# Moving the gelu and its closing table load behind the softmax exponential of slot 5

## The reference

```python
def attn_layer(x, Wqkv, qs, ksc, Wo):
    q, k, v = jnp.split(x @ Wqkv, 3, -1)          # 16 heads of 64
    q = l2norm(q) * qs
    k = l2norm(k) * ksc
    q = q * cos * scale + rotate_half(q) * sin * scale
    k = k * cos * inv + rotate_half(k) * sin * inv
    return local_attention(q, k, v) @ Wo          # windows of 32, softmax over 64 keys

def ffn_layer(x, g, bln, W1, b1, W2, b2):
    hg = layernorm(x, g, bln) @ W1 + b1
    a, gate = jnp.split(hg, 2, -1)                # 341 wide each
    return a * jax.nn.gelu(gate, approximate=False) @ W2 + b2

for i in range(DEPTH):                            # DEPTH = 6
    x = attn_layer(shift_tokens(x), ...) + x
    x = ffn_layer(shift_tokens(x), ...) + x
```

## Time and profile before

| | us |
|---|---|
| median of 3 runs | 4368.58 |
| lowest and highest of them | 4362.37, 4377.15 |
| the profiled execution, its own time | 4373.77 |
| span in that profile | 4372.0 |
| PE busy | 3763.1 |
| DVE busy | 2883.2 |
| ACT busy | 2553.7 |
| POOL busy | 1865.4 |

### The profile page before, as it was taken

How to read it: one execution, slowest core, us unless ns; L and a number is a source line. 1 busy time by engine, 2 the same in 40 slices (tenths; PEclk the granted TensorE clock), 3 DMA queues, 4 the chain that set the end, 5 groups by cost and what they waited for, 6 DMA issues and landing times. The chain is left out here.

```text
span 4372.0 us, 155161 instructions
## 1 busy us (share of the span) xinstructions
PE 3763.1 (86%) x66004; PEld 2803.9 (64%) x66004; DVE 2883.2 (66%) x4808; ACT 2553.7 (58%) x4737; POOL 1865.4 (43%) x1571
## 2 busy tenths in 40 slices
PE   5998699987898987899997899997898897898895
PEld 4997566665666665666665666665666665666663
DVE  3223677776677776777776677776677776677773
ACT  2121566665566665666665666665666665666664
POOL 1011354444444543454444454443454454454451
PEclk9676899999999999999998999999999999999997
DMA  0000110101101101111011110111101101111012
GB/s 27 6 9 23 51 30 26 30 26 36 48 27 30 30 25 41 40 30 31 26 31 41 40 30 25 30 30 37 44 27 29 30 25 41 40 30 30 26 30 68
DMA packets 91938, 139.69 MB, mean 32 GB/s; under 512 B 19465, under 2 KB 40608, under 8 KB 90400
## 3 DMA queue, kind: packets, MB, share of 16 engines
q1 hardware_dynamic: 84778, 129.84, 10.1%
q10 hardware_dynamic: 6518, 0.03, 0.1%
HBM read 28.32 MB, written 4.19 MB: 7 GB/s over the span
## 5 line engine op out<-in xcount | busy, mean ns | idle before, releaser
L1066 POOL TENSOR_TENSOR nat<-ra,rb 128x512 f32<-128x512 f32 x768 | 999.3, 1301 | 1351.7 <-DVE ra L1107 1169.5
L1070 POOL TENSOR_TENSOR nat<-nat,rr 128x512 f32<-128x512 f32 x768 | 814.8, 1061 | 689.8 <-ACT rr L1020 634.7
L1106 DVE TENSOR_TENSOR rb<-ps,tab 128x512 f32<-128x512 f32 x768 | 526.1, 685 | 454.0 <-ACT sq L977 446.7
L783 PE MATMUL ps<-wh,xls 128*128 128x512 f32 x1152 | 614.6, 534 | 217.0 <-PEq L126 188.5
L977 ACT ACTIVATE sq<-ps 128x512 f32<-128x512 f32 x768 | 447.4, 597 | 183.4 <-PE ps L785 145.8
L814 PE MATMUL ps<-kT,qT 64*32 64x64 f32 x24704 | 448.0, 220 | 88.9 <-issue 85.9
L1107 DVE TENSOR_TENSOR ra<-ps,tab 128x512 f32<-128x512 f32 x768 | 522.2, 680 | 0.0
L814 PEld LDWEIGHTS ps<-kT,qT 64*32 64x32 f32 x24704 | 371.2, 106 | 182.5 <-issue 166.1
L795 PE MATMUL ps<-con,nat 128*128 128x128 f32 x3080 | 432.4, 278 | 41.6 <-POOL nat L1070 31.4
L784 PE MATMUL ps<-wl,xhs 128*128 128x512 f32 x1152 | 466.7, 405 | 0.0
L785 PE MATMUL ps<-wh,xhs 128*128 128x512 f32 x1152 | 466.0, 405 | 0.0
(11 more groups left out here) (166 smaller groups left out, 6076.2 us busy)
## 6 DMA issues: line engine op xcount, KB each, us to landing
v<-v SPq DMA_DIRECT2D x192, 396.0 KB, 3.6
v<-v SPq DMA_DIRECT2D x96, 132.0 KB, 3.5
raw<-in_L_ffn_Wqkv SPq DMA_DIRECT2D x7, 1536.0 KB, 6.5
v<-v SPq DMA_DIRECT2D x96, 66.0 KB, 3.2
tab<-in_rotary SPq DMA_DIRECT2D x6, 512.0 KB, 3.3
raw<-in_L_ffn_Wo SPq DMA_DIRECT2D x6, 512.0 KB
xnat<-in_L_attn_hidden_states SPq DMA_DIRECT2D x8, 256.0 KB, 3.7
sT<-so SPq DMA_DIRECT2D x8, 256.0 KB, 2.0
```

The source lines that it names most:

```text
L783: nc.tensor.matmul(dst, al, bh, start=True, stop=False)
L1066: nc.gpsimd.tensor_tensor(nat[:, k, :], ra[:, k, :], rb[:, k, :], ALU.add).then_inc(cur["add"], 1)
L1070: nc.gpsimd.tensor_tensor(nk, nk, rr[:, k, :].unsqueeze(2).broadcast_to([P, 8, DH]), ALU.mult).then_inc(cur["qkn"], 1)
L1106: nc.vector.tensor_tensor(heads8(rb[:, k, :]), heads8(ps[:, bank, :])[:, :, ::-1, :], sin, ALU.mult)
```

## The change

In ScalarE's program, the gelu of slot 5, with the wait for `gx` ahead of it and the table load behind it, moves from in front of the norm's logarithm to behind the softmax exponential of the same slot. Nothing else changes: the same instructions with the same operands.

```diff
@@ -1008,10 +1008,6 @@
-                if i == 5:
-                    act.wait_ge(cur["gx"], NJ)
-                    nc.scalar.activation(gx[:], gx[:], ACT.Gelu).then_inc(cur["gl"], 1)
-                    nc.scalar.preload_act_table_set(LN_EXP)
                 if full:
                     act.wait_ge(cur["g"], i + 1)
                     nc.scalar.activation(nrm[:], nrm[:], ACT.Ln, scale=RN * RN).then_inc(cur["ln"], 1)
@@ -1029,6 +1025,10 @@
                 if live(i, 2):
                     act.wait_ge(cur["sub"], i + 1)
                     nc.scalar.activation(pr[:, i % 2, :], pr[:, i % 2, :], ACT.Exp).then_inc(cur["exp"], 1)
+                if i == 5:
+                    act.wait_ge(cur["gx"], NJ)
+                    nc.scalar.activation(gx[:], gx[:], ACT.Gelu).then_inc(cur["gl"], 1)
+                    nc.scalar.preload_act_table_set(LN_EXP)
```

## The result

Timed side by side, the changed kernel takes 4467.8 us (median of 4 runs, 4464.5 to 4471.9), the one before 4372.9 us (4362.4 to 4377.2). The ratio is 1.0221, with a 95% interval from 1.0199 to 1.0244. Timed once more, later, it was 1.0232 (1.0215 to 1.0249). The kernel is slower by about 95 us, where +82 was forecast. The kernel before stands 4.3 us higher in this timing than the 4368.6 us that the forecast starts from, so the difference is the thing to compare, not the time.

What follows compares the result with a forecast made beforehand. A ring through ScalarE, DVE and PE was taken to bound the kernel, so delays of slot 6's squares count in full: 37.5 + 33 + 11 = +82 us on 4368.6 gives 4451 us, range 4405 to 4500.

Steps and rivals of the forecast that it cites:

- three signs: Wrong if slot 6's squares wait for PE, their delay misses the round distance, or granted clock falls in most rounds.
- What bounds the kernel: Slots 5 and 6: no single engine but a ring; a delay of slot 6's squares meets no slack beyond some tenths.
- the ring: Squares on ScalarE, rotary and sums on DVE, turned output, v and next projections on PE, squares again.
- What the change removes: Slot 5: norms 2.0 us sooner, exponential at 3.39 us instead of 4.92, PE's 1.53 us wait nearly gone; off the ring.
- What it adds, the queue: ScalarE: exponential 0.66, block 4.09, `v` and `pt` 0.94, 5.69 us in sum; slot 6's squares at 9.08, delayed 1.38 us.
- What it adds, the second chain: Gelu, DVE's gated product, PE's projection of q: would allow slot 6's squares at 8.5 us, not setting the end.
- Two kinds of rounds: 28 short rounds (early subtraction) cost 37.5 us; 20 with PE stalled in slot 5's scores cost 33 and 11 us.
- The clock rival: PE's clock falls in its new idle time: 0.81 us in each of 48 rounds, +39 us, 4490; 15 in 100.
- Part given back: PE's stalls without shown cause shrink when PE comes later, giving 4422 or 4433 us; 17 in 100.
- Faster: Squares not waiting for ScalarE, PE keeps its saved wait: 61 us less, 4308; block from 2.71 down; 5 in 100.
- no change: The delay vanishes at each round's end, where engines wait on each other across the loop's jump; 4 in 100.
- The table load: Each load costs only what the block's 4.09 us shows; by the skill's 2.66 us per switch, another 131 us.

Runs made afterwards that it cites:

- up_sooner: Kernel before, with PE's last up-projection of slot 6 moved ahead of slot 5's turned probabilities: ratio 0.9959, timed again 0.9985.
- behind_norms: Against the kernel before, the gelu block stands behind the norm's exponential and ahead of the output copy and softmax exponential: ratio 1.0355.
- defer_load: Changed kernel, with the closing table load moved from behind slot 5's gelu to ahead of slot 6's norm logarithm: ratio 1.0179 to before.
- the two controlled kernels: keep_pe_busy, and the changed kernel with seven short matmuls (32 columns of weights, 16 of data) at the same place: ratios 1.0192 and 1.0240 to before.
- keep_pe_busy: Changed kernel, with 7 unread matmuls of 128x512 added on PE in slot 6 ahead of its wait for the gated product: ratio 1.0192 to before.
- behind_pt: Gelu block one step further on than in the changed kernel, behind the copies of `v` and turned probabilities: ratio 1.0423 to before.

## Why the prediction was right, and where its sizes were off

Two of the three signs that the prediction named as proof against itself showed in part: the squares of slot 6 waited for PE in 14 of 48 rounds (6 in the second profile), and the granted clock fell in 34 (33). That the difference came out within 13 us of the forecast is in part luck: the two terms that the sum left out, the clock and what is given back, have opposite signs.

- *What bounds the kernel.* Right. A delay of slot 6's squares went round the ring: +86 us there were +105 us at the scaled output of slot 7 and +93 at the end. up_sooner shows the same with the other sign in slots 6 and 7.
- *What the change removes.* Right. The exponential is at 3.39 us and the wait at `turn_probs` is gone, and nothing of either is seen on the ring; behind_norms, with early norms alone, is slower still.
- *What it adds, the queue.* Right to 0.01 us in the short rounds: 9.09 for 9.08.
- *What it adds, the second chain.* The statement was that the projection would allow the squares at 8.5 us and does not set the end. For the squares it held in 34 rounds, and defer_load uncovered it at 8.63. In the other 14 it failed: PE's slow projection set them, 0.25 us later than the sum of the steps in 13 of them. For the turned output it failed too. In the rounds in which PE's clock falls, the projections reach the scaled output last, and the chain through the gelu holds the end there.
- *Two kinds of rounds.* Right in size: 28 and 20 before, 27 and 21 after, though not the same rounds. Their sum was put at 81.5 us and measured 85.8. Some 3 to 4 us of the difference are the 14 rounds whose squares waited for PE. PE's idle time of "nearly 3" us in the 20 rounds was wrong: the wait is 2.23 us at most in any round; the stall inside the scores stands apart, ahead of it.
- *The clock rival.* It was set beside the forecast with 0.81 us in each of 48 rounds. It is real but smaller: 17 us on the way to the scaled output in the changed kernel (13 in its second profile), 19 us by the two controlled kernels, and the 3 to 4 us at the squares. It should have been a term of the sum and not a rival, since the prediction itself worked out the idle time of 2 us. The Trainium skill ("TensorE: Matmul & The Clock Gate", Part 1) says that activity releases the throttle; keep_pe_busy agrees, with the clock full in all 48 rounds up to the scaled output of slot 6 and the mean back at 0.938.
- *Part given back.* 12 us were in the first profile, 3 in the second. The mechanism offered, that PE's stalls of unshown cause shrink when PE comes later, is not shown: their total over the transformer fell from 129.6 us (125 stalls) to 119.9 us (118), but only to 124.5 us (120) in the second profile, and it was not tested by itself.
- *Faster, no change.* Faster fell by its own point: the block on the path was 4.09 us and not under 2.71. No change fell because the delay did not vanish at the end of the round: of 105 us there, 93 were left at the end.
- *The table load.* The block takes 4.09 us in its new place too, and with the closing load gone `v` starts 0.09 us ahead of the gelu's end in defer_load (2068.00 against 2066.61 + 1.48). No drain beside the loads shows in either. The Trainium skill ("ScalarE: Activation LUTs", "What ACT_TABLE_LOAD costs") gives 1380 ns of drain with each switch; in this case the measurement decides.

Put together from what was measured, the sum is 86 + 17 + 2 - 12 = +93 us. The first term was worked out ahead and the clock was named beside it; nothing in the rows gave the size of the last.

## What to carry to other kernels

An instruction block that overlaps a wait of its engine is cheap only as far as the wait reaches; before moving it, follow each instruction behind the new place and each waiter for its result to the point where they meet again, and take the later of the two. Where the move leaves TensorE idle, as for the 2.2 us here, read from the granted clock what follows at half speed and put it into the sum, not beside it. A gain of a few tenths of a microsecond in one slot may come back as a stall of the instruction stream elsewhere, so measure the whole, with more rounds than the local gain seems to need.

## What the runs showed of the hardware that was not expected

- PE waits of 2.2 us (after), 3.56 us (behind_pt) and 3.74 us (behind_norms) came with half clock in 34, 48 and 45 of 48 rounds; a wait of 1.53 us (before) did not in 28 rounds. Yet behind a stall of 1.45 us in slot 0 of keep_pe_busy the clock was at half level, so the length of one wait does not decide alone. In the round shown of after, PE's first four matmuls behind the wait still run at full speed and the sixth does not.
- Seven matmuls that nobody reads, put into the idle time, kept the clock full in slots 5 and 6 in all 48 rounds. Whether they gain more than they cost in the whole is open: by the ratios 13 to 17 us, by the profiled executions nothing.
- Fourteen more instructions per round in PE's stream (weight loads and matmuls) moved its stalls out of slot 5 (late exponential in 21 rounds before the edit, in 5 and 6 with it) and into other slots, slot 0 above all, and lengthened the rest of the rounds by 29 to 62 us in sum.
